# A fused GRU and mixture-of-experts kernel: the router's side work placed in other steps of the recurrence

## The reference, cut to what matters

```python
def cell(h, x):
    gi = x @ W_ih + b_ih
    gh = h @ W_hh + b_hh
    i_r, i_z, i_n = jnp.split(gi, 3, axis=-1)
    h_r, h_z, h_n = jnp.split(gh, 3, axis=-1)
    r = jax.nn.sigmoid(i_r + h_r)
    z = jax.nn.sigmoid(i_z + h_z)
    n = jnp.tanh(i_n + r * h_n)
    h_new = (1.0 - z) * n + z * h
    return (h_new, h_new)
...
norm = jnp.maximum(jnp.linalg.norm(x, axis=-1, keepdims=True), 1e-12)
router_logits = x / norm @ router_w
routing_weights = jax.nn.softmax(router_logits.astype(jnp.float32), axis=-1)
rw, selected_experts = jax.lax.top_k(routing_weights, TOP_K)
rw = rw / jnp.sum(rw, axis=-1, keepdims=True)
combine = jnp.sum(jax.nn.one_hot(selected_experts, N_EXPERTS, dtype=rw.dtype) * rw[..., None], axis=1)
for e in range(N_EXPERTS):
    out = out + combine[:, e, None] * (x @ Wa[e] @ Wb[e])
```

## Time and profile before

| | us |
|---|---|
| time, median of 3 runs | 1050.69 (1050.54 to 1051.41) |
| time of the profiled execution | 1050.54 |
| its span in the trace | 1048.7 |
| TensorE matmul busy | 991.4 (95% of the span) |
| VectorE busy | 886.3 (85%) |
| ScalarE busy | 682.5 (65%) |
| GpSimd busy | 328.3 (31%) |

### The profile page before, as it was taken

One profiled execution on the slowest core, in us unless ns is written; L12 is line 12 of the kernel. 1 busy time (PEld: TensorE's weight loads), 2 busy tenths in 40 slices (PEclk: granted clock), 3 DMA queues, 4 the chain that ended last, 5 costly groups with the idle time before them and its releaser, 6 DMA issues.

```text
span 1048.7 us, 63117 instructions
## 1 busy us (share of the span) xinstructions
PE 991.4 (95%) x30603; PEld 742.2 (71%) x21839; DVE 886.3 (85%) x3503; ACT 682.5 (65%) x2762; POOL 328.3 (31%) x792
## 2 busy tenths in 40 slices
PE   4789999999999999999999999999999999999997
PEld 3566777777777777777777777777777777777774
DVE  6889888888888888888888888888888888888886
ACT  7677666666666666666666666666666666666653
POOL 2033323332323332332332333333332333232333
PEclk9999999999999999999999999999999999999999
DMA  8230111111111111111111111111111111110000
GB/s 293 83 91 20 26 31 32 28 27 32 25 33 29 31 26 31 26 32 29 32 25 29 28 31 29 32 25 29 29 30 31 29 28 30 27 29 20 13 8 27
DMA packets 49508, 38.98 MB, mean 37 GB/s; under 512 B 34676, under 2 KB 39112, under 8 KB 49224
## 3 DMA queue, kind: packets, MB, share of 16 engines
q1 hardware_dynamic: 48376, 31.41, 11.1%
q10 hardware_dynamic: 848, 3.54, 1.0%
HBM read 18.94 MB, written 8.39 MB: 26 GB/s over the span
## 4 chain that ended last, share of the span: by engine, by line
PE 80%; DVE 14%; ACT 3%; issue 2%; DMA 1%; ACTq 0%; POOL 0%; DVEq 0%; POOLq 0%
PE gates L974 13%; PE gates L979 10%; PE pairs L869 9%; PE ybank L869 9%; PE nbank L869 9%; PE obank L869 5%; PE pairs L860 5%; PE zbank L860 4%; PE zbank L869 4%; PE nbank L860 4%; PE ybank L860 4%; PE obank L860 2%; DVE pre L765 2%; DVE tr L762 2%; DVE npre L782 1%
## 5 line engine op out<-in xcount | busy, mean ns | idle before, releaser
L620 ACT ACTIVATE rr<-pre 128x64 f32<-128x64 f32 x256 | 65.6, 256 | 242.8 <-DVE pre L765 242.5
L869 PE MATMUL ybank<-hparts,wa 128*128 128x128 f16 x2048 | 213.5, 219 | 0.0
L869 PE MATMUL pairs<-wx,xs 128*32 128x256 f16 x4096 | 209.6, 273 | 0.0
L468 POOL TENSOR_TENSOR y<-y 128x128 f16<-128x128 f32 x256 | 106.6, 437 | 290.9 <-ACT y L669 276.6
L974 PE MATMUL gates<-whh,st 128*32 128x256 f16 x4080 | 158.5, 274 | 38.8 <-DVE st L791 36.9
L869 PEld LDWEIGHTS ybank<-hparts,wa 128*128 128x128 f16 x2048 | 164.9, 98 | 34.1 <-issue 20.6
L860 PE MATMUL ybank<-hparts,wa 128*128 128x128 f16 x1024 | 184.4, 219 | 0.0
L869 PEld LDWEIGHTS pairs<-wx,xs 128*32 128x32 f16 x4096 | 114.6, 97 | 75.6 <-issue 26.5
L762 DVE STREAM_TRANSPOSE tr<-gates 128x256 f32<-128x256 f32 x256 | 115.1, 450 | 58.9 <-PE gates L979 55.7
L979 PE MATMUL gates<-whh,hparts 128*32 128x256 f16 x4080 | 157.9, 273 | 0.0
L860 PE MATMUL pairs<-wx,xs 128*32 128x256 f16 x2048 | 148.0, 273 | 0.0
(11 more groups left out here) (152 smaller groups left out, 2136.6 us busy)
## 6 DMA issues: line engine op xcount, KB each, us to landing
out<-outb SPq DMA_DIRECT2D x63, 128.0 KB
xin<-in_x SPq DMA_DIRECT2D x58, 128.0 KB
wih<-in_L_cond_W_ih ACTq DMA_DIRECT2D x4, 768.0 KB, 7.7
whh<-in_L_cond_W_hh SPq DMA_DIRECT2D x4, 768.0 KB, 11.9
wih<-in_L_ffn_Wb SPq DMA_DIRECT2D x8, 256.0 KB, 2.8
xs<-xh SPq DMA_TRANSPOSE x116, 3.2
wih<-in_L_ffn_Wa SPq DMA_DIRECT2D x4, 256.0 KB, 4.8
whh<-in_L_ffn_Wa SPq DMA_DIRECT2D x4, 256.0 KB, 3.4
```

The lines of the kernel that those rows point to most:

```text
L468: nc.gpsimd.tensor_tensor(y[:, m % YB, 1, :], y32[:, m % 2, :], y[:, m % YB, 0, :], ALU.subtract).then_inc(ylo_ready, 1)
L620: nc.scalar.activation(rr[:, :], pre[:, RG, :, :].rearrange("p k b -> p (k b)"), ACT.Sigmoid, scale=1 / PROD_SCALE).then_inc(r_ready, 1)
L869: return nc.tensor.matmul(out, lhsT, rhs, start=start, stop=stop, skip_group_check=True)
```

## The change

Some of the side work is moved; nothing is added or removed except two waits on GpSimd.

- GpSimd: `gather_states` waits for one step less, so it runs beside position 0 instead of 1. The squares are spread: `fold_squares` is issued at position 1, `add_squares` and the first `less_upper_half` at position 2, the second `less_upper_half` at position 3. The first two get a wait for the step's own state (`both_parts_ready`).
- ScalarE: `read_router` goes from between the first two sigmoids of position 3 to behind that step's two seeds. `weigh` goes from the end of position 3 to position 4, between the tanh and the seeds.
- TensorE: `route` at position 3 stands behind the quarter of the pair, which it no longer replaces; position 4 has three quarters like the other even positions. At even positions the pair's products go ahead of the experts' second products.

```diff
             def gather_states(f, part):
-                pool.wait_ge(both_parts_ready, 2 * ((f + 1) * S + 2))
+                pool.wait_ge(both_parts_ready, 2 * ((f + 1) * S + 1))
...
-            def fold_squares(f):
+            def fold_squares(f, n):
                 pool.wait_ge(sq_ready, f + 1)
+                if n < T:
+                    pool.wait_ge(both_parts_ready, 2 * (n + 2))
...
-            def add_squares(f):
+            def add_squares(f, n):
                 pool.wait_ge(sq_step, f * SQ_STEPS + 1)
                 wait(pool, logits_done, f)
+                if n < T:
+                    pool.wait_ge(both_parts_ready, 2 * (n + 2))
...
             def beside(n):
                 i, s = n // S, n % S
+                if s == 1 and 1 <= i:
+                    fold_squares(i - 1, n)
+                if s == 2 and 1 <= i:
+                    add_squares(i - 1, n)
+                    less_upper_half(i - 1, 0)
+                if s == 3 and 1 <= i:
+                    less_upper_half(i - 1, 1)
                 if s == 0 and 1 <= i:
                     for part in range(2):
                         gather_states(i - 1, part)
-                    fold_squares(i - 1)
-                    add_squares(i - 1)
-                    for part in range(2):
-                        less_upper_half(i - 1, part)
                 if s in (2, 5) and 1 <= i and i + 2 < NB:
                     split_x(i + 2, s // 3, n)
...
                                      scale=1 / PROD_SCALE).then_inc(r_ready, 1)
-                if n % S == 3 and n >= S:
-                    read_router(n // S - 1)
...
                                      scale=1 / PROD_SCALE).then_inc(n_ready, 1)
+                if n % S == 4 and n >= S:
+                    weigh(n // S - 1)
                 if n + 1 < T:
                     seed(n + 1)
                     seed_z(n + 1)
+                if n % S == 3 and n >= S:
+                    read_router(n // S - 1)
...
-                if s == 3 and 1 <= i:
-                    weigh(i - 1)
...
             def wide_step(n):
                 i, s = n // S, n % S
+                pair_ahead(n, (0,))
                 if s == 3 and 1 <= i:
                     route(i - 1)
-                else:
-                    pair_ahead(n, (0,))
...
             def grouped_step(n):
-                i, s = n // S, n % S
+                pair_ahead(n, (2, 3) if n == 0 else (1, 2, 3))
                 if 0 <= n - UP:
                     expert_up_by_tokens(n - UP, n)
                     expert_up_by_tokens(n - UP + 1, n)
-                pair_ahead(n, (2, 3) if n == 0 else range(K) if s == 4 and 1 <= i else (1, 2, 3))
```

More of the change, by code:

```diff
@@ L535, in last_experts @@
             def last_experts():
-                fold_squares(NB - 1)
-                add_squares(NB - 1)
+                fold_squares(NB - 1, T)
+                add_squares(NB - 1, T)
                 for part in range(2):
```

## The result

The changed kernel takes 1057.57 us, median of 4 runs (1056.27 to 1057.89), against 1050.72 for the kernel before: ratio 1.0059, 95% interval 1.0043 to 1.0076. It is slower, by 6.9 us; the forecast was 15 us slower, with a range from 1053 to 1076 that holds the time. The direction came out, and so did which steps get longer and which shorter; the size did not: it is less than half.

The account below looks back on a forecast made before the run. Bounds: TensorE's queue at odd positions and 4, the recurrence's loop at even ones, GpSimd holding VectorE at position 1. Terms: +0.53 us in 29 blocks, -0.3 for two; +15.1 on 1050.54 gives 1065.6, range 1053 to 1076.

Parts of the forecast that it names:

- position 1, the squares gone: Without the squares on GpSimd beside it, position 1 falls from 4.70 to 3.88 us: -0.82 a block.
- position 0, the copies: At position 0 the second copy holds VectorE's addition L770, in a step that pays in full: +0.37 us.
- position 2: `fold_squares` pushes back the two `y`, but VectorE's L765 would still end at +1.82: 0, or 0.22 without cover.
- position 3, the wait for the squares: At position 3 TensorE stands 0.90 us at `route` until the last square, queued behind `split_x`, is done at +2.66.
- quarter moved and `weigh`: Quarter of a pair moved from position 4 to 3, +0.03 us; `weigh` delaying the seeds of position 5, +0.05.
- positions 5 to 7: The steps at positions 5 to 7: no term in the sum apart from `weigh` delaying the seeds of position 5.
- the start of the squares at +0.42: At position 3, `add_squares`, gated by `both_parts_ready`, starts 0.42 us after TensorE's start of the step.
- TensorE's arrival at +1.76: At position 3, TensorE reaches `route` 1.76 us after its start of the step, behind the pair's quarter.
- The rival without the wait: At position 3 TensorE doesn't wait for the squares at `route`: -0.37 us a block, 1039 us; chance 0.12.
- the one in which copies do nothing: Rival at position 0: the copies don't hold VectorE; +0.16 us in 29 blocks, 1054 us; chance 0.12.
- The third, a worse handing out: Rival on the shared interface: both copies pass L765, `y` holds it at position 2; +1.00 in 29 blocks, 1080; chance 0.11.
- `read_router` "nothing": On ScalarE, `read_router` behind the seeds of position 3 lies under the longer step and costs nothing.

Follow-up runs that it names:

- the second experiment: The changed kernel with the copies (`gather_states`) waiting one step more, so they run at the start of position 1 as before the change: 1049.1 us, ratio 0.9984.
- the experiment with the added wait: The changed kernel with one wait more on GpSimd, the last `less_upper_half` waiting for `split_x` ahead of it: 1060.80 us, ratio 1.0100.
- the first experiment: The changed kernel with the last `less_upper_half` moved directly behind the first, ahead of `split_x`: 1055.49 us, ratio 1.0046.
- the new placing: Against the kernel before: GpSimd's copies, squares, `y` and first `split_x` placed anew at positions 1, 2, 3 and 5, `read_router` behind the tanh: 1027.65 us, ratio 0.9785.

## Why the prediction was right or wrong, step by step

| term, us a block | forecast | block 15 |
|---|---|---|
| position 1, the squares gone | -0.82 | -0.82 |
| position 0, the copies | +0.37 | +0.20 |
| position 2 | 0 | +0.01 |
| position 3, the wait for the squares | +0.90 | +0.73 |
| quarter moved and `weigh` | +0.08 | +0.02 |
| positions 5 to 7 | 0 | +0.02 |
| sum of the block | +0.53 | +0.16 |

**Right.** That position 1 was long because GpSimd's squares held VectorE's additions; that copies hold them as well; that position 0 pays in full and 5 to 7 don't; that `split_x` in the queue makes TensorE stand at `route`, 29 times; the start of the squares at +0.42 and TensorE's arrival at +1.76 (484.71 - 482.95, where no wait stood in front of the router). The rival without the wait is out by the new row of waits, the one in which copies do nothing by the second experiment. The third, a worse handing out, is out by its prices: L772 keeps its 0.23 at positions 0 and 2, where it would have been held. But what it rested on, that GpSimd's next instruction can start ahead of VectorE's addition, is what happened, and it made the change cheaper, not dearer.

**Wrong: the handover between GpSimd and VectorE.** From the rows before I had read that "GpSimd's next one starts only when that addition is done (503.46)". There the next instruction, `add_squares`, depended on the one before it, and its 0.08 for the signal ended just when the addition did. The trace of the kernel before held a case against it, in block 1: the copies end at 61.46, L765, which they met, at 61.53, and the next instruction, which doesn't depend on them, had started by then:

```profile
61.43 0.72 POOL L452 TENSOR_TENSOR sq<-sq 128x256 f32<-128x256 f32 x1
```

I carried the reading over to the two places where the next instruction is independent: the second copy and the last square. In the changed kernel the last square starts 0.04 before `split_x` ends, not 0.08 after it, and with the end of the addition as its bound it had been put at +2.11 where it came at +1.95. That is 0.16 of the 0.17 by which the wait was too large: 0.12 at this handover, which the experiment with the added wait puts back, and 0.04 because `split_x` too started before the square ahead of it ended (513.84 against 513.48 + 0.40). At position 0 the second copy ended at +2.29 instead of +2.42: 0.08 for the same reason, 0.05 because the copies too started 0.05 ahead of the end of the `y`. Of the remaining 0.04, 0.02 is the delay of L765 by the first copy, of which L772's 0.23 shows none; the last 0.02 isn't resolved by rows of 0.01.

So the step that failed is the size of two terms: the wait for the squares, put at 0.90 and measured at 0.73, and the copies at position 0, put at 0.37 and measured at 0.20. Both together were 0.34 too large, and 29 x 0.34 is 9.9 us. The miss is 9.0 us against the profiled execution (1056.58) and 8.0 against the median of the runs. What partly offsets the 9.9: over blocks 2 to 29 the changed trace is 5.7 us longer, of which the medians of the eight positions give 4.3; some single steps last 0.1 to 0.7 us more than their median in both traces, 12 of them (3.2 us) after and 8 (1.7 us) before. Why isn't known.

**Wrong, at next to no price here: `read_router` "nothing".** I let it lie under the longer step and named norm and ranking as those who wait for it. TensorE waits for it too, in `expert_down`. In the changed kernel the wait for the squares came first and hid it in blocks 1 to 29. In blocks 30 and 31, where no `split_x` delays the last square, it isn't hidden: position 3 is 4.68 in both, where the forecast's terms give 1.99 + 0.39 + 2.10 = 4.48 for block 30, and with `read_router` behind the tanh it is 4.45 and 4.05. The changed kernel's own trace had a row for it, in block 31:

```profile
1020.95 0.22 PE L876 MATMUL ybank<-hparts,wa 128*128 128x128 f16 x1 [0.74 <-ACT router L663]
```

With the squares early it holds position 3 at the same 4.96.

**What bounds position 3 in the changed kernel**, then, is two waits that end close together. The one for the squares brings TensorE to the second expert at +4.21 (516.73 - 512.52). The router's copy ends there at 516.28 + 0.18 = 516.46; with the 0.14 from the end of the copy to TensorE of the first experiment (515.36 + 0.18 to 515.68), that is +4.08, an estimate. So the squares' earlier place could give 0.13 at most, and moving them delayed the copy by 0.12: TensorE came at +4.20 (515.68 - 511.48). A forecast of what one repair brings goes wrong by 12 us, as mine for the first experiment did.

## What to carry to other kernels

Before a stall on one queue is priced, list every wait in that step, on every engine, by the semaphore and not by the name of the work: the next wait in the same step takes over what the first gives up. A gap between two instructions has a cause of its own (here a signal of 0.08); a number taken from a dependent pair may not be used for an independent one. And where two engines share something, look for the stretch of the loop in which one of them doesn't need it: here the first 1.5 us of a step took the copies and the squares free, and the new placing as a whole, `read_router` included, was worth 23 us against the kernel before.

## What the runs showed of the hardware

- An addition on VectorE with both inputs in SBUF, met by a GpSimd instruction on 128 x 128 elements or more, ends 0.08 us after that instruction: with `fold_squares` it took 0.66 instead of 0.23 and with `add_squares` 0.38 instead of 0.18, with a float16 copy 0.39 instead of 0.18, with `split_x` 0.48 instead of 0.23.
- It need not be served ahead of GpSimd's next instruction (the last square started at 514.47, the addition ended at 514.59), nor does that one become longer: a `less_upper_half` took 0.40 there and 0.40 where no addition met it (513.48).
- A GpSimd instruction that waits for the one before it started 0.08 us after its end (512.94 + 0.46 to 513.48), where independent ones overlap by 0.04 in the records (513.48 + 0.40 against 513.84).
